# Attention: probabilities as stationary operand in plain float32, normalised by query, transposed afterwards

## The reference

```
attn = einsum('bhqd,bhkd->bhqk', query_states, key_states) * SOFTMAX_SCALE
attn = softmax(attn, axis=-1)
out  = einsum('bhqk,bhkd->bhqd', attn, value_states)
out  = out.transpose(0, 2, 1, 3).reshape(b, s, NH * V_DIM)
return out @ wo
```

## Time and profile before

| what | us |
|---|---|
| runs of the kernel | 1203.41 median of 3 (1202.18 to 1204.48) |
| the profiled execution, its own time | 1212.62 |
| its span, first to last instruction | 1210.8 |
| PE busy | 1046.0 (86%) |
| DVE busy | 822.8 (68%) |
| ACT busy | 617.0 (51%) |
| POOL busy | 501.7 (41%) |

### The profile page before, as it was taken

How to read it: one execution, slowest core, us unless ns; L and a number is a source line. 1 busy time by engine, 2 the same in 40 slices (tenths; PEclk the granted TensorE clock), 3 DMA queues, 4 the chain that set the end, 5 groups by cost and what they waited for, 6 DMA issues and landing times.

```text
span 1210.8 us, 24733 instructions
## 1 busy us (share of the span) xinstructions
PE 1046.0 (86%) x6200; PEld 865.9 (72%) x6201; DVE 822.8 (68%) x1750; ACT 617.0 (51%) x1340; POOL 501.7 (41%) x464
## 2 busy tenths in 40 slices
PE   4559999997446999999999999999989739999995
PEld 4537777786434788888888888888778627777784
DVE  6354665544674999999999999999834455566542
ACT  2232433422113888888888888888810123343321
POOL 2532233233233455555555555555412532233332
PEclk9999999999676999999999999999999859999998
DMA  9733544422200011111111000101464464454230
GB/s 241 244 128 67 138 100 100 104 47 27 70 0 1 10 36 36 35 35 35 35 35 34 27 31 31 35 35 35 140 217 144 131 209 96 106 141 102 48 54 11
DMA packets 71562, 95.41 MB, mean 79 GB/s; under 512 B 9600, under 2 KB 48640, under 8 KB 71296
## 3 DMA queue, kind: packets, MB, share of 16 engines
q1 hardware_dynamic: 57216, 78.04, 20.8%
q0 software_dynamic: 14304, 16.87, 7.9%
HBM read 64.37 MB, written 34.43 MB: 82 GB/s over the span
## 4 chain that ended last, share of the span: by engine, by line
PE 73%; issue 10%; DVE 6%; POOL 3%; ACT 3%; DMA 1%; another core or an unknown queue 1%; DVEq 1%; ACTq 0%; SPq 0%; POOLq 0%
PE bank L1537 9%; PE bank L1553 7%; PE bank L1356 6%; PE bank L1354 5%; PE bank L1527 5%; PE bank L1358 5%; PE bank L1554 5%; PE bank L1528 5%; PE bank L1529 5%; PE bank L1339 3%; PE bank L1366 3%; PE bank L1368 3%; PE bank L1367 3%; PE bank L1516 2%; PE bank L1517 2%
## 5 line engine op out<-in xcount | busy, mean ns | idle before, releaser
L811 ACT ACTIVATE shared<-bank,small 128x512 f32<-128x512 f32 x256 | 176.1, 688 | 58.6 <-DVE small L1186 56.3
L1186 DVE TENSOR_REDUCE small<-bank 128x1 f32<-128x512 f32 x256 | 175.3, 685 | 38.8 <-PE bank L1529 28.5
L1216 DVE TENSOR_TENSOR split_rows_and_inner<-bank,shared_split 128x512 fp32r<-128x512 f32 x256 | 174.7, 683 | 7.3 <-ACT shared_split L820 5.9
L762 ACT CAST split_rows_and_inner<-bank 128x512 fp32r<-128x512 f32 x78 | 45.9, 588 | 257.0 <-PE bank L1339 232.0
L1537 PE MATMUL bank<-constants,shared 128*128 128x128 f32 x1024 | 155.7, 274 | 0.9 <-ACT shared L811 0.9
L1553 PE MATMUL bank<-shared_split 128*128 128x256 f32 x512 | 144.1, 304 | 5.5 <-DVE shared L1210 2.3
L820 ACT CAST shared_split<-bank 128x512 fp32r<-128x512 f32 x256 | 147.6, 577 | 1.0 <-PE bank L1537 1.0
L1356 PE MATMUL bank<-expert_weights_low,split_rows_and_inner 128*128 x312 | 144.0, 462 | 0.0
L1358 PE MATMUL bank<-expert_weights_high,split_rows_and_inner 128*128 x312 | 143.0, 458 | 0.0
L1553 PEld LDWEIGHTS bank<-shared_split 128*128 128x128 f32 x512 | 96.2, 188 | 56.8 <-issue 27.9
L1554 PE MATMUL bank<-split_rows_and_inner,shared_split 128*128 128x256 f32 x512 | 132.7, 282 | 0.0
(11 more groups left out here) (191 smaller groups left out, 2480.6 us busy)
## 6 DMA issues: line engine op xcount, KB each, us to landing
expert_weights<-L_ffn_w_kernel SPq DMA_DIRECT2D x32, 512.0 KB
shared<-rows_by_expert SPq DMA_DIRECT2D x78, 129.0 KB, 2.4
expert_weights<-L_ffn_wo_kernel SPq DMA_DIRECT2D x16, 512.0 KB
shared<-inverse_sums SPq DMA_DIRECT2D x64, 128.0 KB, 2.8
attended_transposed<-shared SPq DMA_DIRECT2D x32, 256.0 KB, 2.8
expert_weights<-attended_transposed SPq DMA_DIRECT2D x2, 2048.0 KB, 10.1
shared<-attended_transposed SPq DMA_DIRECT2D x2, 2048.0 KB
rows_by_expert<-empty_rows SPq DMA_DIRECT2D x23, 129.0 KB
```

The costliest lines, as they stand in the source:

```text
L811: nc.scalar.activation(prob[k % 2], bank[k % 4][:, :], ACT.Exp, bias=negmax[:, k % 8:k % 8 + 1], accum_out=psum[par][:, k % 8:k % 8 + 1]). ...
L1186: V.tensor_reduce(negmax[:, k % 8:k % 8 + 1], bank[k % 4][:, :], AX.X, ALU.max, negate=True).then_inc(max_ready, 1)
L1216: V.tensor_tensor(pTl[k // 2 % 2][:, :, at], bank[4 + k % 2][:, :].rearrange("p (c n) -> p c n", c=GT), pTh[k // 2 % 2][:, :, at].bitcast( ...
```

## The change

What it does:

- The probabilities are taken out of the banks once, as plain float32: four of the pair's eight tiles by ACT (`BY_ACT`), four by DVE (`BY_DVE`), each into a buffer of its own (`pT[k]`). The low parts and `high_probs`, `low_probs` are gone.
- `attend` works on one tile at a time: the transposed probabilities are the stationary operand, the values (64 columns, plain float32) the moving one. The result has queries in the rows. It is issued up to five tiles later: tiles 0, 1, 2, 3, 4 in slots 4, 5, 6, 6, 7 of their pair, tiles 5, 6, 7 in slots 0, 1, 2 of the next.
- DVE multiplies all of bank 6 by the inverse sums, which now stand along the rows, in one operation; then four PE transposes (`attended_transpose`) turn it round, and ACT takes it out (`take_attended`). The inverse sums go neither to PE nor through DRAM; `add_lower`, `multiply`, `load_values`, `spread` are gone.
- The two heads alternate tile by tile. The query weights have two buffers, so `load_weights` waits for a use one pair earlier.

```
+PT_WORDS = 8 * GT * P
+BY_ACT, BY_DVE = (0, 1, 4, 7), (2, 3, 5, 6)
...
+        pT = [area(F32_SHARED + o + k * GT * P, [GT, P]) for k in range(8)]
+        values = area(F32_SHARED + o, [B, GT, HD])
...
+        def tile(k):
+            return k % 2, k // 2
+        def wait_pT(eng, p, k):
+            if k in BY_ACT:
+                eng.wait_ge(pT_by_act, p * len(BY_ACT) + BY_ACT.index(k) + 1)
+            else:
+                eng.wait_ge(pT_by_dve, p * len(BY_DVE) + BY_DVE.index(k) + 1)
... POOL
-            def load_weights(p, used):
+            def load_weights(p, par, used):
...
+                nc.gpsimd.tensor_copy(values[:, g, :, :], keys[:, :, HD:2 * HD]).then_inc(v_kept, 1)
+            load_weights(1, 1, None)
...
             def pair(p, par):
                 last = among(p, NPAIR - 1)
                 if not last:
                     rope_sum(p + 1)
                 if not among(p, NPAIR - 2, NPAIR - 1):
+                    load_weights(p + 2, par, p + 1)
                 if not last:
                     rope_lower(p + 1, 1 - par)
... ACT
+            def copy_pT(p, k, first):
+                act.wait_ge(pT_psum, p * 8 + k + 1)
+                if k == BY_ACT[0] and not first:
+                    act.wait_ge(early_psum, p)
+                if k == BY_ACT[3] and not first:
+                    act.wait_ge(o_psum, p)
+                nc.scalar.copy(pT[k].rearrange("p c n -> p (c n)"), bank[4 + k % 2][:, :]).then_inc(pT_by_act, 1)
+            def take_attended(p, par, stored):
+                act.wait_ge(attT_psum, p + 1)
+                if stored is not None:
+                    act.wait_ge(att_stored[par], stored)
+                nc.scalar.copy(att[par], bank[7][:, :]).then_inc(att_ready, 1)
             def pair(p, par, half):
                 for k in range(8):
-                    if k == 2 and not first:
-                        take_output(p - 1, 1 - par, 1)
-                    if k == 6:
-                        take_output(p, par, 0)
                     if not (last and k == 7):
                         exp(s + 1, k + 1, par if k < 7 else 1 - par, first and k < 1)
-                    high_probs(p, k, first)
+                    if k in BY_ACT:
+                        copy_pT(p, k, first)
                     if k in ((3, 4) if first else (2, 3)) and not last:
                         queries_latent(p + 1, 1 - par, k - (3 if first else 2))
                     if k in (3, 4) and not last:
                         queries_rope(p + 1, 1 - par, k - 3)
                     if k == 5 and not first:
-                        take_inverse(p - 1)
+                        take_attended(p - 1, 1 - par, None if among(p, 1, 2) else (half - 1 + par) * 16)
... DVE
+            def take_output(p, par):
+                dve.wait_ge(o_psum, p + 1)
+                dve.wait_ge(pinv_ready, p + 1)
+                if not among(p, 0, 1):
+                    dve.wait_ge(attT_psum, p - 1)
+                V.tensor_tensor(attq[par].rearrange("p (k v) -> p k v", k=8), bank[6][:, :].rearrange("p (k v) -> p k v", k=8),
+                                pinv[par].unsqueeze(2).to_broadcast([P, 8, HD]), ALU.mult).then_inc(attq_sb, 1)
             def pair(p, par):
                 for k in range(8):
-                    if k == 2 and not first:
-                        take_output(p - 1, 1 - par, 1)
-                    if k == 6:
-                        take_output(p, par, 0)
+                    if k == 4 and not first:
+                        take_output(p - 1, 1 - par)
                     if k == 7 and not among(p, NPAIR - 2, NPAIR - 1):
                         ropes(p + 2, 0)
                     if k in ((1, 2) if first else (1,)) and not last:
                         ropes(p + 1, k - 1 if first else 1)
                     if k in (3, 4) and not last and not first:
                         latent_lower(p + 1, 1 - par, k - 3)
-                    if k == 4 and not first:
+                    if k == 2 and not first:
                         invert_sums(p - 1, 1 - par)
                     if not (last and k >= 6):
                         row_max(p * 8 + k + 2, k + 2)
-                    low_probs(p, k)
+                    if k in BY_DVE:
+                        copy_pT(p, k, first)
... PE
+            def attend(p, k, first=False):
+                if k == 0 and not first:
+                    pe.wait_ge(attq_sb, p)
+                wait_pT(pe, p, k)
+                for c in range(GT):
+                    last = mm(bank[6][:, k * HD:(k + 1) * HD], pT[k][:, c, :],
+                              values[:, bass.ds(p // PAIRS, 1), c, :].rearrange("p a n -> p (a n)"),
+                              start=(c == 0), stop=(c == GT - 1))
+                if k == 4:
+                    last.then_inc(early_psum, 1)
+                if k == 7:
+                    last.then_inc(o_psum, 1)
+            def attended_transpose(p, par):
+                pe.wait_ge(attq_sb, p + 1)
+                for j in range(GT):
+                    last = tr(bank[7][:, j * P:(j + 1) * P], attq[par][:, j * P:(j + 1) * P], ident)
+                last.then_inc(attT_psum, 1)
             def pair(p, par):
...
                     if k == 5 and not first:
                         if not last:
                             pe.wait_ge(qz_low, p * 2 + 4)
-                        inverse_transpose(p - 1, 1 - par)
+                        attended_transpose(p - 1, 1 - par)
                     if k == 6 and not among(p, NPAIR - 2, NPAIR - 1):
-                        queries(p + 2, 0)
-                    if k > 1:
-                        attend(p, par, k // 2 - 1, k % 2, first)
-                    elif not first:
-                        attend(p - 1, 1 - par, 3, k)
+                        queries(p + 2, par, 0)
+                    if k < 3 and not first:
+                        attend(p - 1, k + 5)
+                    if k > 3:
+                        attend(p, (0, 1, 2, 4)[k - 4], first)
+                    if k == 6:
+                        attend(p, 3, first)
...
+            for k in (5, 6, 7):
+                attend(NPAIR - 1, k)
+            pe.wait_ge(att_ready, NPAIR - 1)
+            attended_transpose(NPAIR - 1, 1)
```

More of the change, by code:

```diff
@@ L648, in pair @@
                     rope_sum(p + 1)
-                if not among(p, 0, 1):
-                    multiply(p - 2, par, half, None if among(p, 2, 3) else (half - 1) * 16)
                 if not among(p, NPAIR - 2, NPAIR - 1):
-                    load_weights(p + 2, p + 2)
+                    load_weights(p + 2, par, p + 1)
                 if not last:
                     rope_lower(p + 1, 1 - par)
-                if not among(p, 0):
-                    add_lower(p - 1, 1 - par)
-                if not last:
-                    load_values(p + 1, 1 - par, None if among(p, 0) else p * 4)
-            for p in range(4):
-                pair(p, p % 2, p // 2)
-            with pool.Fori(0, (NPAIR - 6) // 2) as i:
-                for v in range(2):
-                    pair(i * 2 + 4 + v, v, i + 2)
-            for p in (NPAIR - 2, NPAIR - 1):
-                pair(p, p % 2, p // 2)
-            multiply(NPAIR - 2, 0, NPAIR // 2, (NPAIR // 2 - 1) * 16)
-            add_lower(NPAIR - 1, 1)
-            multiply(NPAIR - 1, 1, NPAIR // 2, (NPAIR // 2 - 1) * 16)
+            head_pairs(pool, pair)
             pool.wait_ge(veps_ready[2], 1)
@@ L831, in queries_rope, with pair @@
                 nc.scalar.copy(qh[par][hh][rows_], rope[rows_]).then_inc(rope_high, 1)
-            def take_output(p, par, hh):
-                rows_ = slice(hh * HD, (hh + 1) * HD)
-                act.wait_ge(o_psum, p * 4 + hh * 2 + 2)
-                if hh == 0 and not among(p, 0, 1):
-                    act.wait_ge(att_ready, p - 1)
-                nc.scalar.copy(raw[par][rows_], bank[6][rows_, :]).then_inc(raw_sb, 1)
-            def take_inverse(p):
-                act.wait_ge(invT_psum, p + 1)
-                act.wait_ge(inv_stored, p * 16)
-                nc.scalar.copy(invT, bank[7][0:8, 0:P]).then_inc(invT_sb, 1)
-            def pair(p, par):
+            def take_attended(p, par, stored):
[3 more added lines that the diff above has]
+                nc.scalar.copy(att[par], bank[7][:, :]).then_inc(att_ready, 1)
+            def pair(p, par, half):
                 first, last = among(p, 0), among(p, NPAIR - 1)
@@ L868, in _ @@
             exp(0, 0, 0, True)
-            head_pairs(act, pair)
-            take_output(NPAIR - 1, 1, 1)
-            take_inverse(NPAIR - 1)
+            for p in range(4):
+                pair(p, p % 2, p // 2)
+            with act.Fori(0, (NPAIR - 6) // 2) as i:
+                for v in range(2):
+                    pair(i * 2 + 4 + v, v, i + 2)
+            for p in (NPAIR - 2, NPAIR - 1):
+                pair(p, p % 2, p // 2)
+            take_attended(NPAIR - 1, 1, (NPAIR // 2 - 1) * 16)
             for g in range(NG):
@@ L1533, in transposed @@
```

(6 more changed lines are left out.)

150 lines of the change are left out of this document (35 added, 115 removed).

## The result

The changed kernel takes **1312.51 us** in the median of 4 runs (1312.2 to 1313.06); beside it the kernel before took 1203.07 (1202.18 to 1204.48, 4 runs). The ratio is **1.0909** with an interval from 1.089 to 1.0928: 109.4 us slower. The forecast was 1296 with a range from 1262 to 1328. Sign and mechanism came out as foretold; 17 us of the loss were missing from the sum.

A forecast was written before the change was run, and what follows sets the result against it. PE was taken to bound the attention stage. A regular pair would go from 15.50 to 18.5 us, thirty times +90; with +0.8, -1.6 and +3.4 elsewhere, +92.6 on 1203.4 gave 1296 us, range 1262 to 1328.

The forecast's parts named there:

- attend: On PE, per regular pair: 64 matmuls and 64 weight loads, about 0.81 us a tile, 6.6 us for eight tiles.
- attended transposes: On PE, per pair: four plain transposes of the attended tile replace the one of 8 columns, +0.3 us.
- wait for the product: PE ahead of attend 0, until DVE's take_output has read bank 6: 1.1 us a pair, bounds 0 and 2.0.
- PE sets the end: Attention stage: PE busy 461 of 465 us, so every microsecond put on it is paid; relieving other engines gives nothing.
- The row of 8 columns: Profile row used to price attend's instructions: 16 instructions of 8 columns take 1.70 us, 0.106 each.
- Rivals 1 and 5: Attend: weight loads hide (chance 0.05), or calls lower to one instruction (0.03); either way 1170 or about 1203 us.
- Rival 2: PE ahead of attend 0: the added wait is absent or small, -33 us, 1263; chance 0.15.
- Other waits: PE's waits for exponentials, copies and low parts in a pair end before PE asks, so they add nothing.
- Outside the regular pairs: Pair 0 +0.8 us, the start before it -1.6 (weight copy done earlier), pair 31 +3.4; values copied once 0.
- A difference carries over: Whole kernel: profiled execution 1212.62 us, median 1203.41; the predicted difference is added to the median, 1203.4 + 92.6 = 1296.
- Rival 4: PE's clock falls as short matmuls idle the array: some 17 us more a pair, beyond 1700; chance 0.02.
- Rival 3: Attention pairs: more waits or a costlier instruction (0.118 us adds 1 us a pair), 1325 us; chance 0.15.

The follow-up runs named there:

- experiment 1: Changed kernel with DVE's take_output moved from slot 4 to the head of slot 3, ahead of latent_lower(0) and row_max(5); 1289.87 us, ratio 1.0624.
- experiment 4: Changed kernel with probabilities and values as rounded float32r, low parts left out, one instruction and one load a call; 1219.39 us, ratio 1.0040.
- 7: Changed kernel with one of the four attended transposes, three quarters of the attended values left out; 1300.59 us, ratio 1.0826.
- 2: Changed kernel with attend moving 32 of the 64 value columns, half of the attended values left out; 1325.10 us, ratio 1.0916.
- experiment 3: Changed kernel with attend moving the value columns twice, 128 instead of 64, except for the last tile; 1331.05 us, ratio 1.0961.
- 5: Changed kernel with take_output at the head of slot 3 and probabilities and values in float32r, low parts left out; 1193.43 us, ratio 0.9933.
- 6: Changed kernel with the earlier take_output of experiment 1 and all eight copies of probabilities made twice, on ACT and DVE; 1304.36 us, ratio 1.0851.
- 9: Changed kernel with earlier take_output and float32r probabilities and values, plus latent_lower moved behind the maximum and the copy; 1203.14 us, ratio 0.9917.
- experiment 10: Kernel before without the low part of the probabilities (no low_probs or its matmul; values keep theirs); 1173.96 us, ratio 0.9679.
- 8: Kernel before with scores waiting only for their own head's split queries, and take_output one tile earlier, ahead of low_probs; 1195.00 us, ratio 0.9951.
- 11: Kernel before with scores waiting only for their own head's split queries, take_output where it was; 1209.96 us, ratio 0.9970.

## Why the prediction was right, and where it was off

The profile after gives each term of the sum, for one regular pair (us):

```
term                              predicted   measured
transposes and scores, 8 tiles    9.0         9.2   (1.14 to 1.15 a tile)
six query matmuls                 1.4         1.5   (0.55 + 0.47 + 0.47)
attend                            6.6         6.8   (0.81 to 0.84 a tile, 0.94 after the wait, 1.73 for two)
attended transposes               0.4         0.43
wait for the product              1.1         1.24
pair                              18.5        19.1
```

- **PE sets the end: right.** DVE, ACT and POOL lost 102, 71 and 121 us, and within the attention stage nothing came of it; every term put on PE was paid (experiments 1, 4, 7).
- **Attend costs two loads a call at 0.11 us: right.** 2048 instructions; columns between 32 and 128 make almost no difference (2, 3); half the loads take 3.3 us off a pair (4). The row of 8 columns was the right relative. Rivals 1 and 5 are out. A price by the four passes of the Trainium skill's "FP8 and Floating Point Precision", section "TensorE Precision Notes", does not hold here: by it a call of 128 columns would cost an estimated 0.107 us more than one of 64, 3 us a pair in experiment 3, where 0.25 were measured.
- **The wait for the product: right in place and cause**, 1.24 against 1.1. Counted from the transposes of tile 3 (606.25), the forecast had the maximum at 1.34, the copy at 1.95, the product at 2.6 and PE back at 3.4, ready at 2.3; the profile has 1.35, 1.95, 2.67 and 3.52, ready at 2.28. The 0.13 lie in the product's start, 0.72 behind the copy's, and in its end. Rival 2 is out.
- **The term that was mis-sized is the pair's sum of small pieces.** None is off by more than 0.25: attend 0.2, the wait 0.13, transposes and scores 0.1 to 0.2, queries 0.1. I took the best case of each: 0.81 for a tile's attend, worked out as 7 x 0.11 + 0.03, where most tiles take 0.84 and the one behind the wait 0.94; 1.13 for transposes and scores, and 0.23 for a query matmul, read from one stretch, where behind attend it takes 0.32 (601.28 to 601.60). All errors go the same way, and thirty pairs made 0.6 us into 18. (The attended transposes are worked out as +0.3 and stand in the sum as 0.4; 0.43 was measured.)
- **Other waits: right.** No wait of PE for exponentials, copies or low parts between 420 and 960 us of the profile after. Experiments 5, 6 and 9 show how near they stand: each came up once attend or DVE's order was changed.
- **Outside the regular pairs the sum had 2.6 and the profiles have 0.2.** Pair 31 costs 4.0 instead of 3.4, pair 0 0.1 instead of 0.8 (why was not tried), the start -3.4 instead of -1.6, and the stretch behind attention is 0.5 shorter by chance. The start has two parts: the moved weight copy gave 1.9, near the 1.6 foretold; the other 1.6 came with the values, copied once instead of split, which the prediction put at 0. These errors hide 2.4 us of the 18 in the pairs, which is luck.
- **"A difference carries over": right in use.** The profiled execution of before had 8.8 us in the first stage that the medians do not have. The sum was built of differences within the attention stage, which that wait does not touch; a difference of the spans would have been off by 10 us.
- **Clock: right**, a granted clock of 1.00 from pair 1 to pair 31. Rival 4 is out.

Rival 3 was the nearest in time (1325), but by little of its mechanism: no wait beside the foretold one, and 0.108 to 0.112 us an instruction, which made attend 6.8 us a pair and not 7.6. The result lies between the forecast and it, inside the range.

## What to carry to other kernels

With 128x128 stationary operands and 8 to 128 moving columns, count instructions with their weight loads, not columns: at a granted clock of 1.00 each cost about 0.11 us here, and a plain float32 call needs two. The operand that needs fewer 128x128 loads belongs on the stationary side (experiment 10 against 5). Price a repeated unit by the mean of its pieces, those behind a wait among them, and not by the best one: a slip of 3% in a unit that runs thirty times made the error here. Work taken off engines that only wait for the bounding one gives nothing, but the order of their operations at the one place where that engine asks for a buffer was worth 34 of the 109 us.

## What the runs showed that I had not expected

- A float32r matmul with 64 columns took 0.11 us in a series (experiment 4), the same as a plain float32 one, and one with 256 took 0.12 in the kernel before (0.48 / 4): one pass halves the number of instructions of a call and makes none of them shorter.
- DVE's 128x256 operations between buffers, 0.40 us each, took 0.89, 0.75 and 0.70 while POOL split and loaded the values.
- A 512-column matmul directly behind a series of attend lets the next one wait 0.32 us (601.28 to 601.60), and so it does behind the transposes (L1472 at 607.75, L1473 at 608.07); behind another long matmul it is 0.23.
- Taking one wait away let another come up in four of five tries (5, 8, 9, 11; 0.6 us a pair in 5 and 9); only experiment 1 kept its whole gain.
- The kernel before took 1201 to 1203 us in two comparisons and 1213 to 1214 in the two others, with one wait in the first stage as the difference that the traces show: PE idles 12 us ahead of L1456 (L1401 in the changed kernels) in the profiles of before and of experiments 1 to 4 and 9 to 11, and under 1 us in those of after and of experiments 5 to 8, which have 4 us of idle time a little later. What causes it stays open; it wasn't tried.
